# Four full expert tiles chosen ahead and run between the last attention batch and the routing of a decoder layer

## What is computed

```python
x = _layernorm(x + _L0_attn_ref(x, ...), axis=-1)
x = _layernorm(x + _L0_xattn_ref(x, ctx_1024, ctx_1024, ...), axis=-1)
x = _layernorm(x + _L0_ffn_ref(x, ...), axis=-1)

def _L0_ffn_ref(x, Ws, bs, Wg, Wu, Wd):          # D, F, E, K = 256, 688, 8, 2
    logits = xt @ Ws + bs
    topk_w, topk_idx = jax.lax.top_k(logits, K)
    topk_w = jax.nn.softmax(topk_w, axis=-1)
    combine = jnp.sum(jax.nn.one_hot(topk_idx, E, dtype=xt.dtype) * topk_w[..., None], axis=1)
    g = jnp.einsum('td,edf->tef', xt, Wg)
    u = jnp.einsum('td,edf->tef', xt, Wu)
    h = jax.nn.silu(g) * u
    y = jnp.einsum('tef,efd->ted', h, Wd)
    out = jnp.einsum('ted,te->td', y, combine)
```

## Time and profile before

| | |
|---|---|
| time, median of 3 runs | 704.95 us (700.82 to 706.38) |
| time of the profiled execution | 706.33 us |
| its span from first to last instruction | 704.2 us |
| PE busy | 631.8 us (90%) |
| PE weight loads | 536.5 us (76%) |
| DVE, ACT, POOL busy | 374.8, 309.1, 282.1 us |
| transfers | 108.84 MB, mean 155 GB/s |

### The profile page before, as it was taken

How to read it: one execution, slowest core, us unless ns; L and a number is a source line. 1 busy time by engine, 2 the same in 40 slices (tenths; PEclk the granted TensorE clock), 3 DMA queues, 4 the chain that set the end, 5 groups by cost and what they waited for, 6 DMA issues and landing times. The chain is left out here.

```text
span 704.2 us, 16877 instructions
## 1 busy us (share of the span) xinstructions
PE 631.8 (90%) x5894; PEld 536.5 (76%) x5895; DVE 374.8 (53%) x981; ACT 309.1 (44%) x799; POOL 282.1 (40%) x511
## 2 busy tenths in 40 slices
PE   6989887999999998999899864999999999999970
PEld 5878874677777776777677644999999999999960
DVE  2778775777777875787678671222112212221224
ACT  2344424577777776776677631221222122221213
POOL 3345354334333357344934134234333433442220
PEclk9999987899999999999999975999999999999995
DMA  8232203566666664444433017777777778677205
GB/s 249 89 81 62 56 25 111 149 181 190 190 192 189 183 205 114 126 128 128 121 101 100 18 32 264 223 247 213 207 229 234 201 209 244 217 202 235 53 0 186
DMA packets 73665, 108.84 MB, mean 155 GB/s; under 512 B 9786, under 2 KB 51330, under 8 KB 72834
## 3 DMA queue, kind: packets, MB, share of 16 engines
q1 hardware_dynamic: 67458, 100.40, 46.4%
q0 software_dynamic: 6144, 7.61, 6.1%
HBM read 73.25 MB, written 12.44 MB: 122 GB/s over the span
## 5 line engine op out<-in xcount | busy, mean ns | idle before, releaser
L1436 DVE TENSOR_REDUCE cmx<-ps 100x1 f32<-100x361 f32 x256 | 134.5, 531 | 68.4 <-PE ps L949 64.3
L1829 PE MATMUL ps<-xsT,W 128*128 128x128 f32 x1408 | 164.1, 276 | 0.6 <-ACT xsT L1870 0.6
L1829 PEld LDWEIGHTS ps<-xsT,W 128*128 128x128 f32 x1408 | 161.3, 193 | 1.0 <-ACT xsT L1870 1.0
L1226 ACT ACTIVATE cpr<-ps 128x300 f32<-128x300 f32 x256 | 104.6, 419 | 57.7 <-PE ps L960 57.2
L1754 POOL DMA_INDIRECT accd<-y,si x32 | 51.2, 1599 | 110.6 <-DVE y L1979 110.6
L1979 DVE TENSOR_SCALAR y<-ps,wt 128x256 f32<-128x256 f32 x32 | 15.5, 484 | 144.4 <-PE ps L1838 107.5
L949 PE MATMUL ps<-st 96*100 96x361 bf16 x256 | 85.9, 339 | 5.6 <-DVE cmx L1436 2.3
L1838 PE MATMUL ps<-WD,hT 128*128 x384 | 88.3, 380 | 1.4 <-DVE y L1979 1.4
L960 PEld LDWEIGHTS ps<-st 120*128 120x128 bf16 x768 | 63.2, 102 | 31.6 <-issue 8.8
L960 PE MATMUL ps<-st 120*128 120x100 bf16 x768 | 77.1, 209 | 3.3 <-ACT st L1231 1.6
L1838 PEld LDWEIGHTS ps<-WD,hT 128*128 128x128 f32 x384 | 70.5, 190 | 10.0 <-issue 1.8
(11 more groups left out here) (220 smaller groups left out, 1014.4 us busy)
## 6 DMA issues: line engine op xcount, KB each, us to landing
W<-in_wgu SPq DMA_DIRECT2D x32, 1408.0 KB, 6.5
st<-parts SPq DMA_DIRECT2D x192, 115.2 KB, 2.5
WD<-in_wd SPq DMA_DIRECT2D x6, 1024.0 KB, 5.8
cx<-in_ctxT SPq DMA_DIRECT2D x16, 361.0 KB, 5.6
x_sb<-in_x SPq DMA_DIRECT2D x8, 200.0 KB
x1d<-x SPq DMA_DIRECT2D x8, 200.0 KB
x1Td<-x1T SPq DMA_DIRECT2D x8, 200.0 KB, 3.3
x1T_sb<-x1Td SPq DMA_DIRECT2D x16, 100.0 KB, 3.7
```

The costliest lines, as they stand in the source:

```text
L1226: act.activation(pr[:, h % (2 * HG), :], ps[:, B_T + h % 2, 0:NCH * L], ACT.Exp).then_inc(exp_ok, 1)
L1436: dve.tensor_reduce(mx[:, half, hh:hh + 1], ps[0:L, B_S + h % 2, 0:CTX], AX_X, ALU.max).then_inc(max_ok, 1)
L1829: mm = pe.matmul(ps[:, bank(t, part), i * P:(i + 1) * P], columns(t, k, c), xsT[:, t.par, k, :], start=(k == 0), stop=(k == KC - 1))
```

## The change

The two blocks become one program; the experts' part is the class `Experts` (called X in `attention`), its body shared by all engines' streams.

- *Choosing four tiles ahead.* The tokens of batches 0 to 7 (groups 0 and 1) are all placed by step 11. DVE spreads their counts (`spread_full`, step 11), PE counts them against the tiles (`count_full`, step 12), DVE finds the full tiles and PE numbers them (steps 13), DVE takes the first NE = 4 of them (`take_full`, step 14), and PE reads their rows and experts out of the list (`rows_of_full`, step 14). ACT copies each result. `first_tiles` fills the first four columns of `gat`, `sca` and `expert_of`. In the last routing these tiles are subtracted from the used ones (`used`), and the remaining ones are packed into columns 4 to 31. The number of tiles stays 32.
- *Late constants* move from step 15 to step 3 on POOL. Their last one is now a full-tile threshold in place of a fill.
- *Weights.* W0 to W2 are allocated beside the attention's tiles. W0 and W1 are loaded by SP at the start of step 15, W2 and W3 at its end. The load of W0 for expert 0 in step 6 is gone.
- *Gathers.* The first four stand on POOL at the end of step 15.
- *The last tail and the routing* (step 16 and what was ahead of the tiles) are written out on PE and ACT, with gate and up of tiles 0 and 1 and the turns of tiles 0 to 2 between them. ACT changes its table of functions four times instead of twice.
- *Tiles.* Gate, centre and up have one PSUM bank each for all tiles. The load of the expert's number on PE moves into `down`.
- Several semaphores are merged; the order of what they guard is the same.

```diff
+    def spread_full(self, dve):
+
+        dve.wait_ge(self.tot_ok, 2)
+        dve.tensor_copy(self.Mfull[:, :, :], self.Mt[1][:, :].unsqueeze(2).to_broadcast([L, E, VJ])).then_inc(self.full_ok, 1)
...
+    def count_full(self, pe, out):
+        pe.wait_ge(self.full_ok, 1)
+        pe.matmul(out, self.Mfull[:, :, :].rearrange("p e j -> p (e j)"), self.ones[:, 0:1],
+                  start=True, stop=True).then_inc(self.full_mm, 1)
...
+    def take_full(self, dve):
+        dve.wait_ge(self.full_ev, 2)
+        dve.wait_ge(self.full_ok, 3)
+        dve.tensor_scalar(self.fsel[:, :], self.order[0:VT, 0:NE], self.fpos[:, 0:1], self.fullf[:, 0:1], ALU.is_equal,
+                          ALU.mult).then_inc(self.full_ok, 1)
+        dve.tensor_scalar(self.taken[:, :], self.fpos[:, :], float(NE), self.fullf[:, 0:1], ALU.is_lt,
+                          ALU.mult).then_inc(self.full_ok, 1)
...
+    def rows_of_full(self, pe, rows, experts):
+        pe.wait_ge(self.full_ok, 4)
+        pe.wait_ge(self.soft, SOFT[2])
+        pe.matmul(rows, self.listed[0][:, :], self.fsel[:, :], start=True, stop=True)
+        pe.matmul(experts, self.ev16[0:VT, :], self.fsel[:, :], start=True, stop=True).then_inc(self.full_mm, 1)
...
+    B_C, B_Y, B_G, B_U, B_X = 2, 3, 4, 5, 6
...
+    def gate_up(self, pe, t, part, i0, i1):
+
+        if part == 0 and i0 == 0:
+            pe.wait_ge(self.xT_ev, t.n + 1)
+            pe.wait_ge(self.w_in[t.slot], 16 * (t.lap + 1))
+        if i0 == 0:
+            if part == 0:
+                wait(pe, self.sg_ok, 2 * t.n - 1)
+            else:
+                wait(pe, self.h_ok, 2 * t.n - 2 + part)
+        out = self.ps[:, (self.B_G, self.B_C, self.B_U)[part], :]
+        for i in range(i0, i1):
+            c = i + sum(len(p) for p in ORDER[:part])
+            for k in range(KC):
+                mm = pe.matmul(out[:, i * P:(i + 1) * P], self.columns(t, k, c), self.xsT[:, t.par, k, :],
+                               start=(k == 0), stop=(k == KC - 1))
+        if i1 == len(ORDER[part]):
+            mm.then_inc(self.gu_mm, 1)
...
+        def down(t):
+            e = pe.value_load(self.expert_of[0:1, bass.ds(t.n, 1)], min_val=0, max_val=E - 1)
+            wait(pe, self.y_ok, t.n)
+            pe.wait_ge(self.h_ok, 2 * t.n + 2)
+            for c in range(FC):
+                mm = pe.matmul(ps[:, self.B_Y, 0:D], hT[:, t.par, c, :], WD[:, c, bass.ds(e, 1), :],
+                               start=(c == 0), stop=(c == FC - 1))
+            mm.then_inc(self.y_mm, 1)
+
+        def emit(t, n):
+            if n + 1 < TILES:
+                self.gate_up(pe, t + 1, 0, 0, 4)
+            if n == 5:
+                pe.wait_ge(self.routed, 7)
+            down(t - 1)
+            if n + 2 < TILES:
+                self.turn_rows(pe, t + 2)
+            if n + 1 < TILES:
+                self.gate_up(pe, t + 1, 1, 0, 3)
+                self.gate_up(pe, t + 1, 2, 0, 4)
+
+        self.steps(emit, pe)
...
+    def first_tiles(self, dve):
+
+        dve.wait_ge(self.R.full_ev, 3)
+        dve.tensor_scalar(self.gat[:, 0:NE], self.R.frows[:, :], -1.0, None, ALU.add).then_inc(self.R.full_ok, 1)
+        dve.tensor_scalar(self.sca[:, 0:NE], self.R.frows[:, :], -1.0, None, ALU.add).then_inc(self.R.full_ok, 1)
+        dve.tensor_copy(self.expert_of[:, 0:NE], self.R.fexp[:, :]).then_inc(self.R.full_ok, 1)
...
+                    if i == NB - 1:
+                        sp.wait_ge(R.full_ok, 8)
+                        X.weights(sp, Step(0, 0))
+                        X.weights(sp, Step(0, 1))
...
-                    if i == FC:
-                        sp.dma_start(W0[:, :, :], wgu[0, :, :, :].rearrange("q p r -> p q r")).then_inc(R.wd_in, 16)
...
+                    if i == NB - 1:
+                        X.weights(sp, Step(0, 2))
+                        for u in range(2):
+                            sp.wait_ge(kq_in[u], 16 * SLOTS * NB)
+                        sp.wait_ge(t_mm, H * (NB - 1))
+                        sp.wait_ge(v_mm, 2 * NB)
+                        X.weights(sp, Step(0, 3))
...
+                    if i == 3:
+                        R.late_constants(pool)
                     if i == NB - 1:
                         for u in range(2):
                             pool.wait_ge(kq_in[u], 16 * SLOTS * NB)
                         pool.wait_ge(t_mm, H * (NB - 1))
-                        R.late_constants(pool)
+                        pool.wait_ge(v_mm, 2 * NB)
+                        X.constants(pool)
+                        pool.wait_ge(R.x2_out, 32 * GROUPS[1][1])
+                        pool.wait_ge(R.full_ok, 8)
+                        for u in range(4):
+                            X.gather(pool, Step(0, u), GROUPS[1][1] * L)
...
+                        if h == 12 and i == 14:
+                            R.rows_of_full(pe, ps[:, M1, GA], ps[0:1, M1, EX])
...
+                        if h == 12 and i == 12:
+                            R.count_full(pe, ps[0:VT, M1, CN:CN + 1])
+                        if h == 12 and i == 13:
+                            R.number_full(pe, ps[0:VT, M1, PS:PS + 1])
...
+                logits(NB - 2)
+                pe.wait_ge(exp_ok, H * NB - 1)
+                X.turn_rows(pe, Step(0, 0))
+                weigh_values(NB - 1, NG - 1)
+                pe.wait_ge(max_ok, H * NB)
+                pe.wait_ge(mT_ev[1], NB)
+                X.gate_up(pe, Step(0, 0), 0, 0, 2)
+                turn_weighed(NB - 1)
+                pe.wait_ge(exp_ok, H * NB)
+                R.enter_group(pe, 2, lists)
+                X.gate_up(pe, Step(0, 0), 0, 2, 4)
+                turn_attended(NB - 1)
+                X.turn_rows(pe, Step(0, 1))
+                X.gate_up(pe, Step(0, 0), 1, 0, 1)
+                project(NB - 1)
+                X.gate_up(pe, Step(0, 0), 1, 1, 3)
+                R.rank_rows(pe, 3, rank)
+                X.gate_up(pe, Step(0, 0), 2, 0, 4)
+                turn_x2(NB - 1)
+                X.turn_rows(pe, Step(0, 2))
+                logits(NB - 1)
+                X.count_first(pe)
+                X.gate_up(pe, Step(0, 1), 0, 0, 4)
+                for k in range(2 * GROUPS[3][0], 2 * GROUPS[3][1]):
+                    R.enter(pe, k, lists)
+                pe.wait_ge(R.split_ok, 8)
+                R.rank_rows(pe, 4, rank[:, 0:E])
+                X.count_last(pe)
+                X.gate_up(pe, Step(0, 1), 1, 0, 1)
+                X.number_tiles(pe)
+                X.gate_up(pe, Step(0, 1), 1, 1, 3)
+                for k in (2 * NB - 2, 2 * NB - 1):
+                    mm = R.enter(pe, k, lists)
+                mm.then_inc(X.route_mm, 1)
+                X.gate_up(pe, Step(0, 1), 2, 0, 2)
+                X.pack(pe)
+                X.gate_up(pe, Step(0, 1), 2, 2, 4)
+                X.tensor(pe)
...
+                logits_out(NB - 2)
+                X.rows_out(act, Step(0, 0))
+                weighed_out(NB - 1)
+                attended_out(NB - 1)
+                X.rows_out(act, Step(0, 1))
+                R.grown(act, 3)
+                X.warm_up(act, ACT.Silu, 1)
+                X.silus(act, Step(0, 0), 0)
+                X.silus(act, Step(0, 0), 1)
+                x2T_out(NB - 1)
+                logits_out(NB - 1)
+                X.warm_up(act, ACT.Exp, 2)
+                R.grown(act, 4)
+                X.warm_up(act, ACT.Silu, 3)
+                X.rows_out(act, Step(0, 2))
+                X.silus(act, Step(0, 1), 0)
+                X.silus(act, Step(0, 1), 1)
+                X.scalar(act)
...
-        def bank(t, part):
-            return 3 * t.par + part
...
-                    if n >= 1:
-                        leaving = expert(t - 1)
-                    if n + 1 < TILES:
-                        gate_up(t + 1, (0,))
-                    if n >= 1:
-                        down(t - 1, leaving)
-                    if n + 2 < TILES:
-                        turn_rows(t + 2)
-                    if n + 1 < TILES:
-                        gate_up(t + 1, (1, 2))
...
+                X.hidden(dve, Step(0, 0), 1)
+                dve.wait_ge(lg_ev, NB)
...
-                R.scaled(dve, 4, ps[0:L, B_RANK, 0:E])
+                X.hidden(dve, Step(0, 0), 2)
```

810 lines of the change are left out of this document (412 added, 398 removed).

## The result

The changed kernel takes 694.85 us (median of 4 runs, 694.13 to 697.25), the kernel before, on the same chip, 705.66 (4 runs, 700.82 to 710.27). The ratio is 0.9847, with a 95% interval of 0.9809 to 0.9885: 10.8 us less. The profiled execution took 694.28 us, its span is 692.5.

What follows compares the result with a forecast made beforehand. TensorE alone bounds the tiles, 7.72 us each, so they must start earlier: 445.7 - 435.5 = 10.2 us gained, about 9.6 net of small operations, from the median 704.95 to 695.5 us; range 688 to 702.

Steps and rivals of the forecast that it cites:

- Where both kernels stand alike: Steady loop's entry state, reached at 445.7 us in the kernel before; PE's work behind it is the same, gain 445.7 - S.
- S: Time the changed kernel enters its steady tile loop, tiles 0 and 1 having gate and up: 435.5 us.
- T0: PE's first turn of gathered rows, 414.4 us: gather started at 408.1 plus 6.19 us to land.
- the rival of the fast gathers: First gathers land in 2.7 us, T0 at 410.9, gain 13 to 14 us; chance 0.15.
- The hold: PE stands 5.5 us, 408.9 to 414.4, for the gathered rows, with batch 15's remaining work behind.
- T0 to S: PE's stretch up to the steady loop: tile work 11.7, batch and routing work 7.8, waits 1.6 us.
- The waits: PE's waits between T0 and S: 0.8 us at the first count, about 0.7 next, at most 0.4 around packing.
- The clock: PE's granted clock back at its upper level about 4 us after T0, 1.00 from about 420.
- The second rival: PE's clock stays low, all 88 records at 0.213 us, gain 2 to 4; chance 0.20 with longer waits.
- ACT's table loads: Two more on ACT, 1.28 us each, ending near 430.5, costed at nothing; each costs 1.28 if uncovered.
- The register load: PE's load of the expert's number, moved ahead of down: costed at nothing; rival 16 us in 32 tiles, chance 0.06.
- x1b's addition: POOL's add behind the four gathers, done at 416.3, claimed well ahead of the residual.

Runs made afterwards that it cites:

- e3_w2_behind_gather: The changed kernel with SP's loads of W2 and W3 issued only when the first gather has landed: 693.07 us, ratio 0.9806.
- e4_gathers_early: The changed kernel with POOL's fills and four gathers ahead of batch 14's deviation instead of behind it: 691.47 us, ratio 0.9806.
- e6_three_ahead: e4_gathers_early with the fourth gather put back behind batch 14's deviation, three staying ahead: 691.48 us, ratio 0.9802.
- e2_no_interleave: The changed kernel with PE's, ACT's and DVE's work on tiles 0 and 1 all behind the packing: 701.18 us, ratio 0.9931.
- e1_load_ahead: The changed kernel with PE's load of the expert's number back ahead of the next tile's gate products: 693.98 us, ratio 0.9832.

## Why the prediction was right

The forecast was 695.5 us in 688 to 702, and the median is 694.85. Part of that closeness is luck: the forecast gain of 9.6 us was taken from a median of 704.95, and with the fourth run the kernel before stands at 705.66. By the medians the gain is 10.8 us, in the two profiled executions 12.0. The mechanism is the one that was forecast: hold, tile work in the routing's waits, the same loop behind. Point by point:

- **Where both kernels stand alike.** 24 records begin at 433.02, 8 of them are left of tile 1, so S = 433.02 + 8 x 0.112 = 433.9; forecast 435.5. 445.7 - 433.9 = 11.8, and the spans differ by 11.7. So nothing behind S moved: the period is 7.72, as costed. The first down product stands at S plus 1.9, 435.80, forecast 437.
- **T0.** Forecast 414.4, measured 413.59. 0.54 us of the difference is that batch 14 came earlier in this execution, which is scatter. From the gather's issue to the turn 6.07 us, forecast 6.3. T0 did not come at 411, so the rival of the fast gathers is out for this kernel. I took 6.19 because the neighbours were alike; e3_w2_behind_gather shows that they matter: with W2 and W3 held back it is 3.46 us to the use of the rows. One reading was wrong: the issue of W0 and W1 was put at 3.93 us each and that of W3 at about 412, but SyncE issues two loads in 1.65 and 1.72 us when no third follows, and is through with W3 at 409.87. Nothing in the sum hung on it. By the Trainium skill (DMA: Bandwidth & Descriptors, Anatomy of one DMA) it would be some 2.3 us, an estimate from its fit of 2.0 us plus the bytes over 436 GB/s. The run without the loads is 1.2 us above that, nearer than to 6.19, and those with them disagree with it.
- **The hold.** Forecast 5.5, measured 5.17. It was called the price of the change, and e4_gathers_early shows that it is: with no hold 3.5 to 4 us are gained. Not the whole 5.17: there TensorE waits 1.77 us for x of batch 14, whose deviation then stands behind the gathers. Taking that wait away as well brought nothing more in e6_three_ahead, at its lower clock. x2 of batch 15, the sign of what the hold costs, is there at 424.06, forecast 424.8, and in the kernel before 416.74.
- **T0 to S.** Forecast 21.1, measured 20.3. By starts in the timeline, tile work 12.6 us (forecast 11.7), waits 1.8 (1.6), and the rest 6.0 (7.8): the small matmuls follow at 0.05 to 0.16 us and the projection takes 0.87, where I had 0.15 and 1.07. This is the term that was mis-sized, by 1.8 us, with 0.9 and 0.2 the other way. That the sum is off by only 0.8 is luck in part.
- **The waits** stood where they were put: 1.03 at the first count (forecast 0.8), 0.56 at the numbering (0.7), nothing at the packing (0.4), and 0.21 at the logits, which was not forecast.
- **The clock.** Forecast at its upper level about 4 us after T0 and from about 420: by the windows it rose at 418.4, 4.8 us after T0, and is 1.00 in 420 to 435. The second rival did not come; e2_no_interleave shows what it would have looked like, 0.50 from 415 to 430 with TensorE busy 1.26 to 3.98 us of each 5. The tile work is all that was taken out of TensorE's stream there.
- **ACT's table loads** are 1.28 us each and end at 429.54, forecast 430.5, with SiLU of tile 1 right behind at 430.02. No wait of TensorE behind them is put down to ACT, so they cost nothing that the trace shows.

```profile
428.26 1.28 ACT L808 ACT_TABLE_LOAD   x1
429.55 0.20 ACT L808 ACTIVATE warm<-warm 128x1 f32<-128x1 f32 x1
```
- **The register load.** e1_load_ahead: no difference in the period, as forecast.
- **Left open.** The 0.6 us for the small operations in batches 11 to 14 and the up to 0.7 us of the late constants in batch 3 can't be read: the arrival of batch 14 wanders by 2.4 us between two executions of the changed kernel and by 6.8 over all profiles, several times as much.
- **Overlooked.** x1b's addition behind the gathers was called harmless. It is so only as long as TensorE holds: in e2_no_interleave the same addition, at the same time, costs part of the 3.47 us of wait, which is 2.06 in the kernel before. And the forecast did not ask whether the gathers could stand further ahead on POOL, where 6.35 us of idle time lie in front of the deviation.
